# Exchanging parts of the scan, the moments and the memory output, with unread TensorE multiplications in the normalizations and at stage ends

## The reference, cut to what matters

```python
def _layernorm(x, axis=-1, eps=1e-05):
    m = jnp.mean(x, axis=axis, keepdims=True)
    v = jnp.var(x, axis=axis, keepdims=True)
    return (x - m) / jnp.sqrt(v + eps)
...
            for c0 in range(0, S, CHUNK):
                sl = slice(c0, c0 + CHUNK)
                g = _grad_fn(W_state, k[:, sl], v[:, sl]) * GRAD_SCALE
...
                (S_state, W_state), Wtraj = jax.lax.scan(step, (S_state, W_state), xs)
...
                h = jax.nn.silu(jnp.einsum('btd,btod->bto', q[:, sl], W1t))
                outs.append(jnp.einsum('bto,btpo->btp', h, W2t))
            retrieved = jnp.concatenate(outs, axis=1)
            out = retrieved @ Wo.T
            out = out * jax.lax.rsqrt(jnp.mean(out * out, -1, keepdims=True) + EPS) * norm_g
            gate = hidden @ gW.T + gb
            return out * gate
```

## Time and profile before

| | us |
|---|---|
| median of 3 runs | 3175.02 |
| lowest and highest | 3173.93, 3179.1 |
| profiled execution, its own time | 3178.22 |
| its span in the profile | 3176.4 |
| its busy time of PE, DVE, ACT, POOL | 2943.2, 2229.7, 1445.2, 734.3 |
| its mean granted clock of PE | 0.906 of full speed |

### The profile page before, as it was taken

One profiled execution on the slowest core, in us unless ns is written; L12 is line 12 of the kernel. 1 busy time (PEld: TensorE's weight loads), 2 busy tenths in 40 slices (PEclk: granted clock), 3 DMA queues, 4 the chain that ended last, 5 costly groups with the idle time before them and its releaser, 6 DMA issues. The chain is left out here.

```text
span 3176.4 us, 43065 instructions
## 1 busy us (share of the span) xinstructions
PE 2943.2 (93%) x15752; PEld 1821.9 (57%) x15752; DVE 2229.7 (70%) x4543; ACT 1445.2 (45%) x2691; POOL 734.3 (23%) x608
## 2 busy tenths in 40 slices
PE   5999999999986999999999999999999757789699
PEld 3666666666653555555555555555554324455487
DVE  5788888888615877777777777777773577766554
ACT  2666666666631344444444444444444321322243
POOL 1000000000000344444444444444444100055100
PEclk7999999999976899999999999999999867555599
DMA  4112212121005011111111011111100100000000
GB/s 95 26 32 46 49 28 51 26 51 21 1 8 120 1 40 40 41 41 40 34 34 34 20 41 41 40 41 41 28 13 1 36 1 9 1 1 1 17 1 14
DMA packets 40479, 95.81 MB, mean 30 GB/s; under 512 B 12439, under 2 KB 29517, under 8 KB 30541
## 3 DMA queue, kind: packets, MB, share of 16 engines
q1 hardware_dynamic: 40268, 93.07, 13.0%
HBM read 35.11 MB, written 7.34 MB: 13 GB/s over the span
## 5 line engine op out<-in xcount | busy, mean ns | idle before, releaser
L916 ACT ACTIVATE l1a_PT<-l1a_st 128x512 f32<-128x512 f32 x1024 | 597.1, 599 | 759.6 <-PE l1a_st L832 755.6
L933 DVE TENSOR_REDUCE l1a_m<-l1a_aux 128x1 f32<-128x512 f32 x1024 | 667.9, 687 | 125.1 <-PE l1a_aux L794 123.1
L441 DVE TENSOR_REDUCE l0s_mquad<-l0s_mx 128x1 f32<-128x512 f32 x1024 | 635.6, 684 | 169.4 <-PE l0s_mx L309 169.4
L883 POOL TENSOR_TENSOR l1a_acc<-l1a_acc,l1a_PT 128x1024 f32<-128x1024 f32 x224 | 569.3, 2542 | 681.2 <-ACT l1a_PT L916 681.2
L417 ACT ACTIVATE l0s_PT<-l0s_st 128x512 f32<-128x512 f32 x1024 | 528.7, 602 | 236.8 <-PE l0s_st L325 234.1
L845 PE MATMUL l1a_ov<-l1a_PT,l1a_V 128*64 128x512 f32 x2048 | 495.7, 605 | 0.0
L830 PE MATMUL l1a_st<-l1a_QA,l1a_KA 128*128 128x512 f32 x1024 | 447.1, 437 | 2.3 <-issue 2.3
L325 PE MATMUL l0s_st<-l_QS,l_KS 128*128 128x512 f32 x1024 | 438.1, 431 | 3.7 <-ACT l0s_PT L417 3.6
L309 PE MATMUL l0s_mx<-l_KS,l_QS 120*128 120x512 f32 x1024 | 415.6, 412 | 20.6 <-DMA l_KS<-qk_rows 20.6
L832 PE MATMUL l1a_st<-l1a_QB,l1a_KB 65*128 65x512 f32 x1024 | 405.6, 396 | 0.0
L794 PE MATMUL l1a_aux<-l1a_KA,l1a_QA 128*128 128x512 f32 x1024 | 398.6, 437 | 0.8 <-DVE l1a_lo L945 0.8
(11 more groups left out here) (351 smaller groups left out, 2771.1 us busy)
## 6 DMA issues: line engine op xcount, KB each, us to landing
l1a_KA<-l1a_hi SPq DMA_DIRECT2D x32, 512.0 KB, 8.2
l_QS<-qk_rows SPq DMA_DIRECT2D x64, 192.0 KB
l_KS<-qk_rows SPq DMA_DIRECT2D x64, 192.0 KB
l1a_QA<-l1a_hi SPq DMA_DIRECT2D x16, 512.0 KB, 4.5
l1a_QA<-l1a_lo SPq DMA_DIRECT2D x16, 512.0 KB, 8.7
l1a_QB<-l1a_hi SPq DMA_DIRECT2D x16, 512.0 KB, 4.6
l1a_KB<-l1a_lo SPq DMA_DIRECT2D x16, 512.0 KB, 6.5
qk_rows<-l0s_hi SPq DMA_DIRECT2D x64, 64.0 KB, 6.9
```

Source lines behind the costliest of these rows:

```text
L441: nc.vector.tensor_reduce(mquad[:, u % 2, tile, g:g + 1], mx[:, n % MX0, :], axis=AX.X, op=ALU.max).then_inc(mx_free[n % MX0], 1)
L883: nc.gpsimd.tensor_tensor(acc[:, h % 2, 1, :], first, PT[:, g % PT_SLOTS, :], ALU.add).then_inc(added_pool, 1)
L916: nc.scalar.activation(PT[:, g % PT_SLOTS, (u % 2) * CW:(u % 2 + 1) * CW], st[:, u % ST1, :], ACT.Exp, scale=1.0 / float(np.sqrt(HD1))).th ...
L933: nc.vector.tensor_reduce(m4[:, b, q, c:c + 1], src, axis=AX.X, op=ALU.max).then_inc(aux_read, 1)
```

## The change

Five parts.

1. The moments. The mean, the variance and the reciprocal root of a layer norm are now made by DVE alone (class `Moments`): the root by eight small steps from a bit pattern, no longer with ACT. For r = 0, 1, 2 and 7 this is done chunk by chunk in the block before, behind each addition into X (`moments.block`); for r = 3 to 6 it stays in the normalization.
2. Loading. X comes in four transfers, and DVE makes the moments of each chunk ahead of clearing `QS`.
3. Unread multiplications. `norm_stage` for r from 1 begins with two PE multiplications of 512 columns into a bank that nobody reads, and has one of 256 columns behind every second turned tile, seven in all. `keep_busy` adds four of 512 columns at the ends of `token_major_out` and `l0_ffn`, and two at those of `l1_ffn` and `l2_attention`.
4. The scan. `hh` and `y2` move one iteration forward (`hh` of c-1, `y2` of c-2), as do `h2a` and `h2c`; on DVE `h2` stands ahead of `gn`, and `m2` ahead of the first state. One iteration at the end goes.
5. The memory output. `Wo` and `norm_g` are loaded for `l3_prepare`, which multiplies the gate's weights by `norm_g`; ACT squares and sums straight from PSUM; the root comes in two halves; one multiplication by root and gate takes the place of two.

```diff
-            sp.dma_start(X[:, :, :], x_dram.rearrange("b (t p) d -> p (b t) d", p=P)).then_inc(x_loaded, 16)
-            sp.wait_ge(x_loaded, 16)
+            tiles = x_dram.rearrange("b (t p) d -> p (b t) d", p=P)
+            for c in range(NC):
+                at = slice(TPC * c, TPC * (c + 1))
+                sp.dma_start(X[:, at, :], tiles[:, at, :]).then_inc(x_loaded[c], 16)
 
...
         @block.vector
         def _(dve):
+            for c in range(NC):
+                dve.wait_ge(x_loaded[c], 16)
+                moments.block(dve, c)
             nc.vector.memset(QS[:, :, :].bitcast(F32), 0.0)
...
+def quartic_rsqrt(nc, dve, link, v, work, out):
+
+    r0, t, qa, qb, rough = work
+    link(nc.vector.tensor_scalar(r0.bitcast(I32), v.bitcast(I32), -0.5, NORM_BITS, ALU.mult, ALU.add))
+    link(nc.vector.tensor_tensor(t, r0, r0, ALU.mult))
+    link(nc.vector.tensor_tensor(t, t, v, ALU.mult))
+    link.open(nc.vector.scalar_tensor_tensor(qa, t, NORM_A[0], t, op0=ALU.add, op1=ALU.mult))
+    qa_at = link.count
+    link.open(nc.vector.scalar_tensor_tensor(qb, t, NORM_B[0], t, op0=ALU.add, op1=ALU.mult))
+    dve.wait_ge(link.sem, qa_at)
+    link(nc.vector.scalar_tensor_tensor(rough, qa, NORM_A[1], r0, op0=ALU.add, op1=ALU.mult))
+    link(nc.vector.scalar_tensor_tensor(out, qb, NORM_B[1], rough, op0=ALU.add, op1=ALU.mult))
...
+class Moments:
...
+    def sums(self, dve, c):
+
+        nc = self.nc
+        self.order.engine = dve
+        for t in range(TPC * c, TPC * (c + 1)):
+            self.order.open(nc.vector.bn_stats(self.stats[:, t, :], self.X[:, t, :]))
+        for t in range(TPC * c, TPC * (c + 1)):
+            dve.wait_ge(self.order.sem, self.order.count - TPC + 1)
+            self.order.open(nc.vector.bn_aggr(self.mv[:, t, :], self.stats[:, t, :]))
+
+    def roots(self, dve, first, last):
+
+        nc, link = self.nc, self.order
+        link.engine = dve
+        at = slice(TPC * first, TPC * last)
+        v = self.work[:, 0, at]
+        dve.wait_ge(link.sem, link.count)
+        link(nc.vector.tensor_scalar(v, self.mv[:, at, 1], LN_EPS, NORM_LEAD ** -2, ALU.add, ALU.mult))
+        quartic_rsqrt(nc, dve, link, v, [self.work[:, i, at] for i in range(1, 6)], self.rstd[:, at])
+
+    def block(self, dve, c):
+
+        self.sums(dve, c)
+        if c >= NC - 2:
+            self.roots(dve, 0 if c == NC - 2 else c, c + 1)
+
+
+LATE_MOMENTS = (3, 4, 5, 6)
+
+
+def keep_busy(nc, bank, ident, xnT, n):
+
+    for i in range(n):
+        nc.tensor.matmul(bank, ident[:, :], xnT[:, CW * (i % NC):CW * (i % NC + 1)], start=True, stop=True)
 
...
             @block.vector
             def _(dve):
+                if r in LATE_MOMENTS:
+                    for c in range(NC):
+                        moments.sums(dve, c)
+                    moments.roots(dve, 0, NC)
                 for t in range(NT):
...
-                    nc.vector.tensor_scalar(xn[:, t, :], X[:, t, :], mv[:, t, 0:1], rstd[:, t:t + 1],
+                    nc.vector.tensor_scalar(xn[:, t, :], X[:, t, :], moments.mv[:, t, 0:1], moments.rstd[:, t:t + 1],
                                             ALU.subtract, ALU.mult).then_inc(s["normed"], 1)
 
             @block.scalar
             def _(act):
-                act.wait_ge(s["var_done"], r + 1)
-                nc.scalar.activation(std[:, :], rstd[:, :], ACT.Sqrt).then_inc(s["std_done"], 1)
                 for c in range(NC):
                     act.wait_ge(s["transposed"], r * NT + TPC * (c + 1))
                     nc.scalar.activation(xnT[:, c * CW:(c + 1) * CW], tp[:, c, :], ACT.Copy)
 
             @block.tensor
             def _(pe):
+                filler = X[:, 0:TPC, :].rearrange("p t d -> p (t d)")
+                for n in range(2 if r else 0):
+                    nc.tensor.matmul(spare[:, :], ident[:, :], filler, start=True, stop=True)
                 for t in range(NT):
                     pe.wait_ge(s["normed"], r * NT + t + 1)
                     nc.tensor.transpose(tp[:, t // TPC, (t % TPC) * P:(t % TPC + 1) * P], xn[:, t, :],
                                         ident[:, :]).then_inc(s["transposed"], 1)
+                    if t % 2 and t < NT - 1 and r:
+                        nc.tensor.matmul(spare[:, 0:2 * D], ident[:, :], filler[:, 0:2 * D], start=True, stop=True)
...
                 dve.wait_ge(done, TPC * (c + 1))
                 x = X[:, TPC * c:TPC * (c + 1), :].rearrange("p t d -> p (t d)")
-                nc.vector.tensor_tensor(x, po[:, c, :], x, ALU.add)
+                nc.vector.tensor_tensor(x, po[:, c, :], x, ALU.add).then_inc(added, 1)
+                dve.wait_ge(added, c + 1)
+                moments.block(dve, c)
...
                 nc.tensor.matmul(o, ones[0:1, 0:P], bo[0:1, :], start=False, stop=True).then_inc(done, 1)
+            keep_busy(nc, tp[:, 0, :], ident, vT, 4)
...
             pe.wait_ge(gate_lin, NC)
+            pe.wait_ge(gain_done, 2)
...
+            nc.vector.tensor_tensor(gW[:, :], gW[:, :], ng[:, :], ALU.mult).then_inc(gain_done, 1)
+            nc.vector.tensor_tensor(gb[:, :], gb[:, :], ng[0:1, :], ALU.mult).then_inc(gain_done, 1)
...
         @block.tensor
         def _(pe):
-            for c in range(NCH + 3):
+            for c in range(NCH + 2):
                 if c < NCH:
...
-                if 0 <= c - 2 < NCH:
-                    o = c - 2
+                if 0 <= c - 1 < NCH:
+                    o = c - 1
                     pe.wait_ge(s["h2_ready"], o + 1)
                     pe.wait_ge(s["tok_done"], 3 * min(c + 1, NCH))
                     if o >= 1:
                         pe.wait_ge(s["m2_ready"], o)
                     nc.tensor.matmul(hh, hd[:, o % 3, :], h2[:, :], start=True, stop=True).then_inc(s["hh_full"], 1)
...
-                if 0 <= c - 3:
-                    o = c - 3
+                if 0 <= c - 2:
+                    o = c - 2
...
-                if c >= 2:
-                    o = c - 2
+                if c >= 1:
+                    o = c - 1
                     pool.wait_ge(s["h2_ready"], o + 1)
...
+                link(nc.vector.tensor_scalar(side[:, :], pn, hn[:, :], EPS3 ** 2 / NORM_SCALE, ALU.mult, ALU.max))
+                if c >= 1:
+                    second_activation(c - 1)
+                dve.wait_ge(s["zn_full"], c + 1)
...
+                if c >= 1:
+                    second_scores(c - 1)
...
-        @block.sync
-        def _(sp):
-            sp.dma_start(Wo[:, :], W["L3_attn_Wo"]).then_inc(loaded.sem, 16)
-            sp.dma_start(ng[:, :], row_of(W["L3_attn_norm_g"]).broadcast_to([P, D])).then_inc(loaded.sem, 16)
-
...
         @block.tensor
         def _(pe):
-            pe.wait_ge(loaded.sem, loaded.all)
             for t in range(NT):
                 nc.tensor.matmul(po[:, t // TPC, (t % TPC) * D:(t % TPC + 1) * D], T["retr"][:, t * P:(t + 1) * P],
-                                 Wo[:, :], start=True, stop=True).then_inc(o_full, 1)
+                                 T["Wo"][:, :], start=True, stop=True).then_inc(o_full, 1)
 
         @block.scalar
         def _(act):
-            for c in range(NC):
-                act.wait_ge(o_full, TPC * (c + 1))
-                nc.scalar.activation(o[:, TPC * c:TPC * (c + 1), :], po[:, c, :].rearrange("p (t d) -> p t d", d=D),
-                                     ACT.Copy).then_inc(o_out, 1)
-            act.wait_ge(ms_done, 1)
-            nc.scalar.activation(rs[:, :], ms[:, :], ACT.Sqrt).then_inc(root_done, 1)
+            for t in range(NT):
+                act.wait_ge(o_full, TPC * (t // TPC + 1))
+                nc.scalar.activation(sq[:, t, :], po[:, t // TPC, (t % TPC) * D:(t % TPC + 1) * D], ACT.Square,
+                                     accum_out=ms[:, t:t + 1]).then_inc(ms_done, 1)
 
         @block.vector
         def _(dve):
             link = Chain(dve, dve_order)
-            dve.wait_ge(loaded.sem, loaded.all)
...
+            for half in range(2):
+                at = slice(NT // 2 * half, NT // 2 * (half + 1))
+                dve.wait_ge(ms_done, NT // 2 * (half + 1))
+                v = work[:, 0, at]
+                link(nc.vector.tensor_scalar(v, ms[:, at], NORM_LEAD ** -2 / D, EPS3 * NORM_LEAD ** -2, ALU.mult, ALU.add))
+                quartic_rsqrt(nc, dve, link, v, [work[:, i, at] for i in range(1, 6)], inv[:, at])
+                for c in range(NC // 2 * half, NC // 2 * (half + 1)):
+                    for t in range(TPC * c, TPC * (c + 1)):
+                        link.open(nc.vector.scalar_tensor_tensor(o[:, t, :], po[:, c, (t % TPC) * D:(t % TPC + 1) * D],
+                                                                 inv[:, t:t + 1], T["gate"][:, t, :],
+                                                                 op0=ALU.mult, op1=ALU.mult))
+                    dve.wait_ge(dve_order, link.count)
+                    ot = o[:, TPC * c:TPC * (c + 1), :].rearrange("p t d -> p (t d)")
```

(4 more changed lines are left out.)

279 lines of the change are left out of this document (121 added, 158 removed).

## The result

| | before | changed |
|---|---|---|
| median of 20 runs of each, side by side | 3176.39 | 3170.65 |
| lowest and highest | 3171.51, 3180.82 | 3166.81, 3173.03 |
| profiled execution, its span | 3178.22, 3176.4 | 3171.54, 3169.8 |
| busy PE, DVE, ACT, POOL | 2943.2, 2229.7, 1445.2, 734.3 | 2970.6, 2237.1, 1429.1, 734.6 |
| mean granted clock | 0.906 | 0.918 |

The ratio is 0.9983, with an interval of 0.9976 to 0.9989: 5.4 us faster by the ratio, 5.7 by the difference of the medians. That is clear of noise, but under the 0.2% that the prediction set as its bound. The prediction had forecast 5.5 us. As will be seen, most of its terms were near, and those that were off cancelled, which was luck.

The account below looks back on a forecast made before the run. The prediction took a chunk-to-chunk chain to bound the scan and a DVE chain each normalization. Its gains and costs summed to 5.5 us won, giving 3169.5 us against the median, with an 8-in-10 range of 3152 to 3182.

Parts of the forecast that it names:

- scan: Scan: `y1` no longer waits for `h2` (8.6 us), one readout iteration goes (2.8 us); together +11.4 us.
- memory output, r = 7 with its unread work: Memory output to `n_xn`: 25.1 us against 31.3, +6.0; unread multiplications of r = 7: -1.5 us.
- loading: Loading block: clearing `QS` now follows the last moments and delays `n_xn` to about 17.1 from 13.7: -3.3 us.
- r = 1 and 2: First two layers: r = 1 wins 1.5 us through the clock, r = 2 wins 0.5 us.
- r = 3 to 6: Unread work in these normalizations and at block ends, net of the clock: -1.3, -2.3, -4.0 and -1.5 us.
- The rival with another wait: Scan: another wait replaces `y1`'s, a chunk stays at 5.65 us; 8.6 us less won, 3178 us; chance 0.12.
- the price: Normalizations: unread multiplications make PE the bound; tiles 7.5 us with the clock rising midway, -3.2 us each.
- the return: Next layers start at full clock: +2.9 us behind normalization 7, an estimated +1.9 behind 3, 4 and 6.
- The 8-column products behind r = 5: Behind normalization 5: 10.3 us at clock 0.52, full of 8-column multiplications that did not raise it; little return.
- that all engines meet at the block's end: End of the block for r = 4: `keep_busy` (1.8 us at full clock) outlasts the last addition (0.69); another -1.0 us.
- The low clock: Late normalizations and r = 1: clock stays at half through the tiles, 33 us worse, 3202 us; chance 0.14.
- The held clock: Late normalizations: unread work keeps the clock full, costing 0.8 us each, +5.1 behind r = 5; 3153 us; chance 0.22.

Follow-up runs that it names:

- no_unread: The changed kernel without any unread multiplication, neither in the normalizations nor at the stage ends: 3150.11 us, 0.9920.
- combined: The changed kernel without any unread multiplication and with `QS` cleared on POOL: 3147.91 us, 0.9907; run again, 3146.86 us, 0.9907.
- late_seventh: The `combined` kernel with the moments of r = 7 back in the normalization: 3140.75 us, 0.9893.
- late_moments: The `no_unread` kernel with the moments of r = 1, 2 and 7 back in the normalization: 3153.1 us, 0.9926.
- root_only: The kernel before with only the root of the eight normalizations made by DVE in eight small steps: 3170.45 us, 0.9985.

## Why the prediction was right, and where it was wrong

The total was right to 0.1 or 0.2 us (5.5 forecast, 5.4 by the ratio, 5.7 by the medians); in the profiled executions 6.6 us of span are won. Each row is the time from the first matmul of one stage to that of the next, named by what lies between; the last column is the range over the kernels without unread work that share the stage's code (`no_unread`, `combined` twice, `late_seventh`, `late_moments`):

| between the first matmuls of | before | changed | without unread work |
|---|---|---|---|
| `l0o_tp` and `l0f_up` (r = 1) | 35.1 | 35.8 | 31.4 to 31.9 |
| `l0f_up` and layer 3 (r = 2) | 56.3 | 53.2 | 51.0 to 53.5 |
| its attention and layer 4 (r = 3) | 1496.3 | 1500.7 | 1495.5 to 1496.2 |
| layer 4 and layer 5 (r = 4) | 48.8 | 50.7 | 46.7 to 46.8 |
| layer 5 and layer 6 (r = 5) | 106.4 | 109.1 | 103.3 to 105.9 |
| `l2f_lg` and the next product | 6.8 | 3.7 | 4.3 to 6.8 |
| layer 6 and `l3_prepare` (r = 6) | 57.2 | 60.8 | 57.3 to 57.4 |
| `l3_prepare` and the first `z` | 76.0 | 72.8 | 72.8 to 74.6 |
| first `z` and the memory output | 194.3 | 179.8 | 179.5 to 180.1 |
| memory output and layer 8 (r = 7) | 35.0 | 35.1 | 30.9 (28.8 with late moments) |
| layer 8, to the end | 177.7 | 177.4 | 175.6 to 178.5 |

(`late_moments` stands outside the first two rows, of which it has 35.2 and 56.2.) By the steps of the prediction:

| step | forecast | measured |
|---|---|---|
| scan | +11.4 | +10.9 |
| memory output, r = 7 with its unread work | +4.5 | +3.4 |
| loading | -3.3 | -4.1 |
| r = 1 and 2 | +2.0 | +2.4 |
| r = 3 to 6 | -9.1 | -6.2 |

*The scan* went as worked out: the wait of `y1` gone, nothing late behind it, the chunk of 5.33 us. Of its row's 14.5 us, 3.6 are the transfer's wait ahead of the output. The rival with another wait fell, by the changed kernel's chunk and by the scan alone.

*The memory output* was sized at 25.1 us up to `n_xn` and took 23.6. ACT's squares let DVE begin 5.0 us after PE's start (2962.16 less 2957.20), the forecast's 3.6 + 1.4, so nearly all of the 1.5 us is in the estimate of DVE's chunks (18.2 us, from 2962.16 to 2980.31, against 19.5). That the moments lie here costs 2.1 us, which the prediction had not weighed against leaving them in the normalization.

*Loading* cost a microsecond more than forecast: besides the 5.18 us of clearing there is 1.34 us of idle ahead of it. With POOL clearing, all of it comes back.

*The unread multiplications.* Their price and their return can be read apart. In the next table the price stands in the time from the last addition to `n_xn` (where `keep_busy` and the moments are) and in that from `n_xn` to the next layer's first product (where the tiles are), the return in the first run behind it. Each cell has the kernel before, the changed one, and those without unread work (`no_unread`, `combined` twice, `late_seventh`; in the last column also `late_moments`):

| r | last addition to `n_xn` | `n_xn` to the next product | first run of the next layer |
|---|---|---|---|
| 1 | 6.17, 4.70, 3.12 | 5.67, 7.66, 5.50 to 5.65 | 9.20, 7.11, 7.11 to 9.41 |
| 2 | 6.17, 3.12, 3.12 | 9.27, 11.27, 9.11 to 9.26 | 27.9, 27.7, 27.3 to 27.7 |
| 3 | 6.20, 6.08, 6.07 | 6.39, 9.91, 6.45 to 6.54 | 7.11, 6.10, 6.10 |
| 4 | 6.36, 7.03, 6.06 | 5.66, 8.63, 5.65 | 5.66, 3.92, 3.92 to 5.28 |
| 5 | 6.20, 9.04, 6.07 | 5.66, 8.16, 5.50 to 5.66 | 6.97, 3.85, 4.47 to 6.97 |
| 6 | 6.20, 6.08, 6.07 | 5.66, 9.10, 5.65 | 9.02, 7.08, 7.08 to 8.88 |
| 7 | 6.17, 3.11, 3.11 (late moments 6.07) | 7.74, 12.02, 7.75 | 11.75, 11.75, 11.2 to 11.8 |

The price was sized well where it was named: for the tiles of r = 3 to 7 the forecast has 15.8 us and the table 16.7. For r = 1 and 2 the forecast names none, and they cost 2.1 us each. Over all places the changed kernel pays some 26 us against the kernels without unread work, 5.5 of them in the first column and 21 in the second. *The step that failed is the return*: "In return the next layer starts at full clock", worth 10.7 us in sum (2.1, 1.9 three times, 2.9). It was counted against the half clock of one profiled execution of the kernel before, as if without the unread work every such layer started at half. The kernels without it start at full clock too, in some executions or in all (r = 3), and so does `root_only` behind r = 1, which has neither unread work nor early moments (7.10 us). Against them only some 5 us come back of the 26, which fits the 20 that the medians show.

Behind normalization 3 shows only the first moments. The window that follows there, in the kernel before:

```profile
2476.00:2478.90 2.90, 2.90 (x5) 1.21 (x4) 1.28 (x2) 0.60 (x1) 0.00 (x0) 0.50 0.00 0
```

The clock rose behind the tiles and fell again within the first run; layer 4 takes 36.8 us from its first product to its last addition there, and 35.1 in the changed kernel and in all without unread work. Why it never fell in the latter is not settled. So against this kernel before, a return of 1.7 us did come behind normalization 3, with 1.9 forecast; it lies in the row of r = 4, and the row of r = 3 has the tiles' 3.5 us and another 0.9 in the attention. Behind normalization 7 the return of 2.9 us didn't come. Windows of the changed kernel there:

```profile
2985.50:2989.30 3.80, 3.80 (x24) 2.99 (x22) 0.00 (x0) 1.72 (x3) 0.00 (x0) 1.00 0.17 52
2989.40:2991.80 2.40, 0.00 (x0) 0.00 (x0) 0.00 (x0) 2.13 (x5) 0.89 (x1) 0.98 0.00 0
2992.30:2998.60 6.30, 6.27 (x18) 5.13 (x19) 0.81 (x2) 1.54 (x4) 3.60 (x3) 0.51 0.00 0
```

The clock had risen among the tiles, as forecast; then PE stood idle for 3 us until POOL had `l3f_xl`, and started the next layer at half clock, as in the earlier trace rows. I had looked at the clock of the layer's start and not at what PE does ahead of it. The tiles' own price for r = 7, forecast at 4.4, was 4.2 (35.1 less 30.9).

*What cancelled it* were terms that were too small or missing. The moments of r = 1 were forecast at some 3.3 us and win 3.0 (6.17 to 3.12, in `late_moments` 6.07 to 3.12). Those of r = 2 win as much, where the forecast let most of it vanish in the next layer's wait; but that layer starts 9.1 to 9.3 us after `n_xn` in either case. The 8-column products behind r = 5 gave 3.1 us that were not forecast, and DVE's chunks in the memory output 1.4. And the root, whose step said "no longer with ACT", was costed at nothing beyond its small steps. The kernel before has 21 table loads of ACT, the one with the root on DVE alone 9, the changed kernel 8: seven of the normalizations load for their root, and five of the layers behind must load their own table again. The group of lines of the kernel before:

```profile
L174 ACT ACT_TABLE_LOAD x7 | 9.0, 1283 | 69.4 <-PEq L523 20.8 <-PEq L1145 18.7 <-PEq L587 12.3
```

One of the twelve loads that `root_only` is rid of stands on the chain, the 1.28 us among the gates of `l3_prepare` (from the first product there to the first of the gates' products, 22.4 us before and 21.2 with the root alone). The steps of the root themselves are 0.1 us shorter in a normalization (6.17 to 6.07 from the last addition to `n_xn`; 0.3 in r = 4), together some 1.1. The other loads are hidden or nearly so: those of the normalizations end 3.2 us or more ahead of the root that they serve, those of layers 4 and 6 end 2.3 and 6.8 us ahead of their next function, that of the third attention ends 0.9 us ahead of the exponential, which waits for DVE, and that of layer 1 puts off the first copy by 0.3 us at most. That r = 5's row is 1.3 us shorter with the root alone (105.1) comes from the clock: the first products of the scores there take 4.30 us instead of 5.49. So 2.4 of the 5.3 us are shown, and the other 2.9 are not: they lie in stages where the clock's rise moves from execution to execution. The Trainium skill's page "ScalarE: Activation LUTs", "Table sets: the hidden batching unit", says that functions of different sets cost a load each when they alternate, and puts two at 5.3 us. The trace agrees on the reloads, but not on their time: the load among the gates starts 0.02 us after one activation ends, and the next starts 0.01 us after it, so it costs 1.28 us.

*r = 5.* The prediction took the 8-column products behind it as work that does not raise the clock. They ran at full clock in the changed kernel. Its windows of the tiles of normalization 5 and of those products, and its timeline from `keep_busy` on:

```profile
2632.40:2636.40 4.00, 4.00 (x15) 3.21 (x16) 3.74 (x15) 0.65 (x2) 0.00 (x0) 0.61 0.00 0
...
2640.10:2643.80 3.70, 3.69 (x32) 3.70 (x33) 0.00 (x0) 0.00 (x0) 0.00 (x0) 0.96 0.02 4
```

```profile
2622.11 3.78 PE L184 MATMUL l2a_sc<-top_xnT,top_ident 128*128 128x512 f32 x4
2622.22 0.69 DVE L1290 TENSOR_TENSOR top_X<-l2a_po,top_X 128x512 f32<-128x512 f32 x1 [5.95 <-PE l2a_po L1224]
...
2626.19 0.87 DVE L156 BATCH_NORM_STATS2 top_stats<-top_X 128x6 f32<-128x128 f32 x4 [3.28 <-PEq L1201]
...
2631.95 4.19 DVE L214 TENSOR_SCALAR n_xn<-top_X,top_mv,top_rstd 128x128 f32<-128x128 f32 x16
...
2640.11 3.85 PE L1385 MATMUL l2f_lg<-l2f_rw,top_xnT 128*128 128x8 f32 x32 [0.93 <-PEq L202]
```

The 32 products take 3.85 us instead of 6.97, 3.1 us given back. Without unread work the same run took 4.5 to 7.0 us, by execution. The second fence shows `keep_busy`'s price: DVE has added at 2622.9, and the block ends 3 us later, when PE is through, at half clock. That step, that all engines meet at the block's end, held.

*The low clock*, the slower rival, fell: in each normalization that the windows above show, the clock rose among the tiles. *The held clock* fell too: it had 0.8 us for a normalization's unread work, and the tiles of r = 3 to 7 took 2.5 to 4.3 us more. Of the 5.1 us that it had behind r = 5, 3.1 came.

Against this stand the runs of single parts. By the medians scan -10.5, root -5.3 and unread work +19.2 make +3.4; the change measured -5.7, so early moments, output and loading together gave 9.1 us (10.7 if all is taken by the ratios). None of these three was run alone on the kernel before. The profiled executions show some 24 us for the unread work (the changed column less the middle of the last one) where the medians have 20; I trust the medians for the size and the traces for the place.

## What to carry to other kernels

Work that only warms an engine must be weighed against the kernel without it, and against more than one execution of that, since real work raises the clock at the same place some of the time; here it cost some 26 us where it stood and 20 net. Work can move into an earlier block for less than its duration only where its engine waits there (r = 1, 2, 4, 5), and is dearer where that engine is the bound (r = 7). And a removed operation is to be costed by what it forces elsewhere: a function of another table can be paid for in the next stage. To see whether it is, lay the two timelines side by side, with the load and without: one reload here cost its 1.28 us, and one that looked the same cost nothing.

## What was unexpected on the chip

- 16 turned tiles in a row, at 0.50 for 3.3 us, were followed by 1.00 for the next 8.7 us, with no other matmul between the tiles and the rise. The first run there took 7.11 us in two executions of this code; in three others the clock rose only within that run.
- In the 2.4 us of an idle PE the clock was still at 0.98 (2989.4 to 2991.8), and 0.51 in the 6.3 us of work that came next. In the kernel before it fell from 1.00 to 0.50 in the midst of layer 4's first run (2476.0 to 2478.9), with PE busy from 2474.3 on.
- POOL's MEMSET of 128 x 6144 took 5.22 us beside DVE's stats, and both kept their durations (0.87 us for four stats in either kernel).
- The same kernel, profiled twice, took 3136.7 and 3147.5 us of span. The stages that differ are the short ones behind a pause of PE (51.0 or 53.5, 103.3 or 105.9, 5.5 or 6.8), the start (22.2 or 24.0) and the last layer (175.6 or 178.5). `l3_prepare`, with the same code, was started at full clock in `late_seventh` and at half in both of these, 1.7 us apart over the first run of 16.
